# A feed-forward stage with W1 as a seven-product block algorithm and W2 summed in PSUM

## The reference

```python
h = jax.nn.gelu(flat_x @ W1 + b1)          # flat_x 1024 x 512, W1 512 x 2048
y = h @ W2                                 # W2 2048 x 512
y = jnp.nan_to_num(y, nan=0.0, posinf=0.0, neginf=0.0)
return y.reshape(orig_shape) + b2
x = x + _L0_ffn_ref(_layernorm(x, axis=-1), ...)
```

## Time and profile before

| what | value |
|---|---|
| time, median of 3 runs | 2129.53 us (2128.24 to 2131.55) |
| the profiled execution, its own time | 2129.44 us |
| its span, first to last instruction | 2127.5 us |
| mean granted TensorE clock | 0.994 |
| TensorE busy | 2072.3 us, 97% of the span |
| VectorE / ScalarE / GpSimd busy | 1500.6 / 1016.8 / 548.4 us |
| feed-forward products | 1926.20 to 2112.06 us |

### The profile page before, as it was taken

The page is one execution under the profiler, slowest core; times in us unless marked ns, Lnnn a source line. Parts: engine busy times, 40 slices in busy tenths (PEclk is TensorE's granted clock), DMA queues, the critical chain, the costliest instruction groups (busy, mean ns, idle before and its releaser), DMA issues.

```text
span 2127.5 us, 33928 instructions
## 1 busy us (share of the span) xinstructions
PE 2072.3 (97%) x11620; PEld 1785.9 (84%) x11620; DVE 1500.6 (71%) x2365; ACT 1016.8 (48%) x2232; POOL 548.4 (26%) x428
## 2 busy tenths in 40 slices
PE   8999999999999999999899999999999999989996
PEld 6888888888888888888788888888888888877885
DVE  6777777777777777777766666666666666677776
ACT  3555555555555555555544444444444444443331
POOL 2222122212221222221222222222222222213223
PEclk9999999999999999999999999999999999999998
DMA  7000000000000000011011111111111111010111
GB/s 234 16 21 16 15 21 20 15 15 20 20 15 15 20 20 20 10 50 40 31 59 43 42 39 36 40 38 41 42 42 42 42 42 42 23 35 25 49 44 50
DMA packets 44162, 76.90 MB, mean 36 GB/s; under 512 B 7378, under 2 KB 13650, under 8 KB 43602
## 3 DMA queue, kind: packets, MB, share of 16 engines
q1 hardware_dynamic: 44114, 76.25, 11.9%
HBM read 74.13 MB, written 2.10 MB: 36 GB/s over the span
## 4 chain that ended last, share of the span: by engine, by line
PE 87%; DVE 6%; issue 3%; ACT 2%; SPq 1%; DMA 0%; DVEq 0%; ACTq 0%
PE bank L1085 22%; PE bank L1087 21%; PE bank L1086 21%; PE bank L1154 9%; PE bank L1200 6%; PE bank L1268 1%; PE bank L1353 1%; PE bank L1352 1%; PE bank L1269 1%; PE bank L1327 1%; DVE negmax L870 1%; DVE V_lo L864 1%; DVE pT_lo L908 1%; DVE q_lo L902 1%; DVE K_lo L860 0%
## 5 line engine op out<-in xcount | busy, mean ns | idle before, releaser
L880 DVE SCALAR_TENSOR_TENSOR xacc<-bank,rinv,xacc 128x512 f32<-128x512 f32 x512 | 376.1, 746 | 71.1 <-PE bank L1087 71.1
L486 ACT ACTIVATE pT_hi<-bank 128x512 fp32r<-128x512 f32 x320 | 190.7, 597 | 202.5 <-PE bank L1200 202.3
L870 DVE TENSOR_REDUCE negmax<-bank 128x1 f32<-128x640 f32 x256 | 210.2, 822 | 36.7 <-PE bank L1154 29.6
L540 ACT ACTIVATE prob<-bank,negmax 128x640 f32<-128x640 f32 x256 | 202.5, 791 | 66.8 <-DVE negmax L870 66.8
L908 DVE TENSOR_TENSOR pT_lo<-bank,pT_hi 128x512 fp32r<-128x512 f32 x320 | 217.9, 681 | 2.4 <-ACT pT_hi L486 2.4
L1200 PE MATMUL bank<-ident,prob 128*128 128x128 f32 x1280 | 191.3, 272 | 0.0
L1200 PEld LDWEIGHTS bank<-ident,prob 128*128 128x128 f32 x1280 | 159.4, 140 | 19.0
L383 POOL TENSOR_TENSOR wo_lo<-wo_raw,wo_hi 128x512 fp32r<-128x512 f32 x32 | 41.4, 1295 | 430.6 <-ACT wo_hi L486 430.6
L626 ACT ACTIVATE xprob<-xscore,negmax 128x128 f32<-128x128 f32 x256 | 99.5, 391 | 95.2 <-DVE negmax L961 95.2
L1085 PE MATMUL bank<-xwv_hi,cT_hi 128*128 128x256 f32 x512 | 143.4, 280 | 1.4 <-DVE xV_lo L928 1.4
L1086 PE MATMUL bank<-xwv_lo,cT_hi 128*128 128x256 f32 x512 | 143.1, 280 | 0.0
(11 more groups left out here) (171 smaller groups left out, 5909.0 us busy)
## 6 DMA issues: line engine op xcount, KB each, us to landing
wq_raw<-in_wq SPq DMA_DIRECT2D x32, 256.0 KB, 2.6
wo_raw<-in_wo SPq DMA_DIRECT2D x32, 256.0 KB, 2.6
xwv_raw<-in_xwv SPq DMA_DIRECT2D x16, 512.0 KB, 3.5
xwk_raw<-in_xwk SPq DMA_DIRECT2D x32, 256.0 KB, 3.7
xwq_raw<-in_xwq SPq DMA_DIRECT2D x32, 256.0 KB, 3.5
xwo_raw<-in_xwo SPq DMA_DIRECT2D x32, 256.0 KB, 2.7
w_raw<-in_w SPq DMA_DIRECT2D x32, 256.0 KB, 2.6
xacc<-in_x SPq DMA_DIRECT2D x8, 256.0 KB, 5.2
```

The costliest lines, as they stand in the source:

```text
L486: return s.activation(dst, src, ACT.Copy)
L540: s.activation(prob[:, slot, i, :].rearrange("p (a t) -> p a t", a=2), S_bank[i % 2], ACT.Exp, bias=negmax[:, slot, i:i + 1], scale=1.0, a ...
L870: v.tensor_reduce(negmax[:, slot, i:i + 1], S_bank[i % 2], mybir.AxisListType.XY, ALU.max, negate=True).then_inc(a["max"], 1)
L880: v.scalar_tensor_tensor(xacc[:, 4 * half + i, :], M, rinv[:, k, i:i + 1], xacc[:, 4 * half + i, :], ALU.mult, ALU.add).then_inc(sems["y"], 1)
```

## The change

The 1024 tokens are two halves X1, X2 and the 2048 hidden units eight groups (g) of two blocks; the 512 features are two halves of two blocks. The 2x2 block product of a group is made from seven half-size products P1 to P7 (`product`, six matmuls each) in place of eight: 42 matmuls in place of 48. For this the kernel makes sums and differences of the weights on GpSimd (`late_sums`, four operations of 128x256 for a group) and of the transposed x on VectorE (four of 128x1024), and their halves: for each group ScalarE copies a high half of 128x1280 (`late_hi`) and GpSimd makes a low half of 128x1280 (`late_lo`), in two slots. VectorE adds the products: `u2`, `u3`, `u4` and then the four results `c11`, `c21` (first half of the tokens), `c12`, `c22` (second half).

P1 and P2 of four groups are made ahead, while the second half of the layer norm runs. The main part has four groups with P1, P2 of a later group and two blocks of W2 (66 matmuls each), then three of 42 matmuls, then the last.

W2: in the first half of the tokens each block of hidden units is added to four PSUM banks that stay open over all 16 blocks (`y0`); there is no `yacc`. The hidden units of the second half are kept in SBUF (`hid1`), W2 is loaded and split a second time (`again`, `again_hi`, `again_lo`), and the last 192 matmuls go token tile by token tile. W2 has four slots for its halves and two for its raw blocks, and its low halves are made by VectorE (`second_lo`; the first two by GpSimd). The result of a tile is finished by VectorE alone, tile by tile (`finish`). A gelu on one column right after the layer norm's last square root loads the gelu table there. The 16 pieces of b1 are loaded at once; the second `spin` of the stage has 6 calls in place of 18.

```diff
-FUNITS = 2 * NF
+NG = NF // 2
+HALF_S = [0, 1, 2, 3, 4, 6, 8, 10]
+LATE_S = [5, 7, 9, 11, 12, 13, 14, 15]
+Y_ORDER = [0, 2, 4, 6, 8, 1, 10, 3, 12, 5, 14, 7, 9, 11, 13, 15]
...
+            def second(s_):
+                if s_ >= 2:
+                    sp.wait_ge(f["w2hi"], f0["w2hi"] + s_ - 1)
+                    sp.wait_ge(f["w2lo"], f0["w2lo"] + s_ - 1)
+                sp.dma_start(w2_raw[:, s_ % 2], w2[Y_ORDER[s_]]).then_inc(s_w2raw[s_ % 2], 16)
...
+            for g in range(NG):
+                for s_ in (7 + 2 * g, 8 + 2 * g):
+                    if s_ < NF:
+                        second(s_)
+                if g + 5 < NG:
+                    early(g + 5)
+                if g + 2 < NG:
+                    late_weights(g + 2)
+                if g == 4:
+                    sp.wait_ge(f["P2"], f0["P2"] + NG)
+                    for n in range(4):
+                        again(n)
...
+            def late_sums(n):
+
+                w = wl_f[n % 2]
+                pool.wait_ge(s_wlraw[n % 2], 16 * (n // 2 + 1))
+                if n >= 2:
+                    pool.wait_ge(f["wlhi"], f0["wlhi"] + n - 1)
+                    pool.wait_ge(f["wllo"], f0["wllo"] + n - 1)
+                g.tensor_tensor(w[:, 4], w[:, 2], w[:, 3], ALU.add).then_inc(f["S0"], 1)
+                g.tensor_tensor(w[:, 6], w[:, 0], w[:, 2], ALU.subtract)
+                pool.wait_ge(f["S0"], f0["S0"] + 2 * n + 1)
+                g.tensor_tensor(w[:, 5], w[:, 4], w[:, 0], ALU.subtract).then_inc(f["S0"], 1)
+                pool.wait_ge(f["S0"], f0["S0"] + 2 * n + 2)
+                g.tensor_tensor(w[:, 7], w[:, 1], w[:, 5], ALU.subtract).then_inc(f["S"], 1)
+
+            def late_lo(n):
+                pool.wait_ge(f["wlhi"], f0["wlhi"] + n + 1)
+                g.tensor_tensor(wl_lo[:, n % 2], wl_f[n % 2][:, 3:8], wl_hi[:, n % 2], ALU.subtract).then_inc(f["wllo"], 1)
+
...
+            for n in range(NG):
+                if n + 1 < NG:
+                    late_lo(n + 1)
+                if n + 5 < NG:
+                    early_lo(n + 5)
+                if n + 2 < NG:
+                    late_sums(n + 2)
+                if n < 4:
+                    bias(2 * n)
+                    bias(2 * n + 1)
...
+            def second_hi(s_):
+                if s_ >= 4:
+                    act.wait_ge(f["y0"], f0["y0"] + s_ - 3)
+                raw_split(w2_hi[:, s_ % 4], w2_raw[:, s_ % 2], s_w2raw[s_ % 2], 16 * (s_ // 2 + 1), f["w2hi"])
...
+            def late_hi(g):
+                act.wait_ge(f["S"], f0["S"] + g + 1)
+                if g >= 2:
+                    act.wait_ge(f["P4"], f0["P4"] + g - 1)
+                copy(wl_hi[:, g % 2], wl_f[g % 2][:, 3:8]).then_inc(f["wlhi"], 1)
...
+            def p1_copy(g):
+                act.wait_ge(f["P1"], f0["P1"] + g + 1)
+                if g >= 5:
+                    act.wait_ge(f["u4"], f0["u4"] + g - 4)
+                    act.wait_ge(f["u3"], f0["u3"] + g - 4)
+                copy(part[:, g % 5], E_bank[0]).then_inc(f["p1"], 1)
...
+            act.wait_ge(s_b1, 16 * NF)
+            s.activation(nrm[:, 4, 0:1], nrm[:, 1, 0:1], ACT.Gelu_apprx_tanh, bias=b1_sb[:, 0:1], scale=1.0)
...
+            for g in range(NG):
+                if g + 1 < NG:
+                    late_hi(g + 1)
+                for s_ in (5 + 2 * g, 6 + 2 * g):
+                    if s_ < NF:
+                        second_hi(s_)
+                if g + 4 < NG:
+                    p1_copy(g + 4)
+                if g + 1 == NG:
+                    hidden_late(g)
+                hidden_second(g, "c22", "g22", 2 * g + 1, late[:, 2])
+                if g + 4 < NG:
+                    hidden_early(g + 4)
+                if g + 5 < NG:
+                    early_hi(g + 5)
+                hidden_second(g, "c12", "g12", 2 * g, late[:, 1])
+                if g + 1 < NG:
+                    hidden_late(g)
+
...
+            def second_lo(s_):
+                dve.wait_ge(f["w2hi"], f0["w2hi"] + s_ + 1)
+                if s_ == 2:
+                    dve.wait_ge(f["w2lo"], f0["w2lo"] + 2)
+                v.tensor_tensor(w2_lo[:, s_ % 4], w2_raw[:, s_ % 2], w2_hi[:, s_ % 4], ALU.subtract)                 .then_inc(f["w2lo"], 1)
...
+            for g in range(NG - 1):
+                for s_ in (5 + 2 * g, 6 + 2 * g):
+                    if s_ < NF:
+                        second_lo(s_)
+                u2(g)
+                u4(g)
+                u3(g)
+                c22(g)
+                if g + 4 < NG:
+                    c11(g + 4)
+                    h_lo(HALF_S[g + 4])
+                c12(g)
+                c21(g)
+                h_lo(LATE_S[g])
...
+            def finish(b, y):
+                if b >= 2:
+                    dve.wait_ge(f["fin"], f0["fin"] + b - 1)
+                v.tensor_scalar(finite[:, b % 2], y, 0.0, 0.0, ALU.mult, ALU.is_equal).then_inc(f["finite"], 1)
+                if b == 0:
+                    dve.wait_ge(s_xb, B)
+                v.tensor_tensor(ysum[:, b % 2], y, xacc[:, b, :], ALU.add).then_inc(f["sum"], 1)
+                dve.wait_ge(f["finite"], f0["finite"] + b + 1)
+                dve.wait_ge(f["sum"], f0["sum"] + b + 1)
+                v.copy_predicated(xacc[:, b, :], finite[:, b % 2], ysum[:, b % 2]).then_inc(f["fin"], 1)
...
+            def product(dst, w, m):
+                for ch in range(2):
+                    last = mm3(dst, [z[:, ch, :] for z in w], [z[:, ch, :] for z in m], ch == 0, ch == 1)
+                return last
...
+            def p7(g):
+                if g == 0:
+                    pe.wait_ge(f["Tlo"], f0["Tlo"] + 3)
+                if g < 4:
+                    pe.wait_ge(f["u2"], f0["u2"] + g + 1)
+                else:
+                    pe.wait_ge(f["c21"], f0["c21"] + g)
+                product(L_bank, late_w(g, 3), xs(1)).then_inc(f["P7"], 1)
...
+            for g in range(4):
+                fill = 3 if g == 0 else LATE_S[g - 1]
+                p6(g)
+                y0(fill, FIRST)
+                p5(g)
+                p1(g + 4)
+                p7(g)
+                p2(g + 4)
+                p3(g)
+                y0(fill, LAST)
+                p4(g)
+                y0(HALF_S[g + 4], EVERY)
+            p6(4)
...
+            p6(4)
+            for g in range(4, NG - 1):
+                p5(g)
+                p7(g)
+                p6(g + 1)
+                y0(LATE_S[g - 1], FIRST)
+                p3(g)
+                y0(LATE_S[g - 1], LAST)
+                p4(g)
...
+            for t_ in range(4):
+                for n in range(NF):
+                    if n % 4 == 0:
+                        pe.wait_ge(f["g1lo"], f0["g1lo"] + 4 * t_ + n // 4 + 1)
+                    if t_ == 0:
+                        if n % 3 == 2:
+                            pe.wait_ge(f["alo2"], f0["alo2"] + n // 3 + 1)
+                        else:
+                            pe.wait_ge(f["alo"], f0["alo"] + n - n // 3 + 1)
+                    last = mm3(Y1_bank[t_], [z[:, t_ % 2, n, :] for z in (hid1_hi, hid1_lo)],
+                               [z[:, n, :] for z in (w2all_hi, w2all_lo)], n == 0, n == NF - 1)
+                last.then_inc(f["y1"], 1)
```

609 lines of the change are left out of this document (439 added, 170 removed), and 3 rows, old and new, of the table f_after.

## The result

The changed kernel takes 2139.85 us (median of 4 runs, 2138.28 to 2140.75), the kernel before 2129.80 (4 runs, 2128.24 to 2131.55): a ratio of 1.005, with a 95% interval from 1.0038 to 1.0063. It is slower by about 10 us. Forecast were 2137.5 us, in a range from 2121 to 2146.

A forecast was written before the change was run, and what follows sets the result against it. TensorE's matmuls were taken as the bound. Terms -11.2 + 10.3 + 5.7 + 8.0 + 4.6 + 1.4, then -10.2 at the end, gave +8.6 (+8.1 as laid out): 2137.5 us, ratio 1.004, range 2121 to 2146.

The forecast's parts named there:

- The saving of 11.2 us: TensorE in the feed-forward stage: eight groups save 6 matmuls each, 48 x 0.233 us, -11.2 us.
- The end: Behind the last matmul: only one tile left to finish, about 2.2 us in place of 12.46, -10.2 us.
- The port: VectorE operations on two SBUF tiles wait for the GpSimd operation under way, up to 2.97 us for 128x1280.
- short waits: Rival, chance 0.20: VectorE gets through within the 1.24 us that rows show, 2129.5 us, no change.
- The rival with VectorE first at the port: Ramp and groups 1 to 3: VectorE isn't held behind GpSimd, up to 15.7 us less, 2121.8 us, faster; chance 0.25.
- The ramp: Stage start to end of group 0: chained copies, low halves and port waits, P7(0) idle 5.0 us; +10.3 us.
- The early load's price: In the ramp: the early gelu table load on ScalarE makes TensorE wait ahead of P1(1), 1.5 us.
- Groups 1 to 3: P7 waits 1.9 us for u2, behind second_lo and late_lo, in each of three groups; +5.7 us.
- Groups 4 to 6: P6 of the next group waits 3.65 us for late_lo, in groups 5 and 6; with c22's delays +8.0 us.
- The clock: TensorE's clock after the two idle times of 3.65 us: between nothing and 1.4 us each, half taken, +1.4 us.
- a colder clock: Rival, chance 0.10: every wait over 1.8 us costs 1.4 us at half clock; +7.0 us, 2144.5 us.
- The second half: Second half of the tokens: P7(7) waits 0.8 us, W2's reload through four slots adds 3.8 us; +4.6 us.

The follow-up runs named there:

- e11: Changed kernel with GpSimd's late_lo cut into three instructions, P6 waiting for all three; 2132.70 us against 2139.85.
- e6: Changed kernel with GpSimd's late_lo as three instructions, each with its own signal, P6 waiting only for the first; 2121.54 us against 2139.85.
- e4: Changed kernel without the early one-column gelu; 216.95 us from cross-attention's last matmul to the kernel's last, against 218.41.
- e10: e9 without the early one-column gelu that loads the gelu table; median 2110.24 us, against 2111.25.
- e1: Changed kernel with VectorE running u2, u4, u3 and c22 ahead of W2's low halves (second_lo); median 3.1 us shorter, not distinguishable from none.
- e2: Changed kernel with ScalarE's late_hi for groups 6 and 7 ahead of hidden_late; cross-attention's last matmul to the last one 5.2 us shorter.
- e3: Changed kernel with each W2 block (0 to 11) of the second pass used for two row blocks; last cross-attention matmul to last matmul 219.16 us, against 218.41.
- e12: The kernel before, profiled again with no edit; cross-attention's last matmul to the last one 197.36 us, against 198.95 in its first profile.
- e9: e8 with late_lo in three pieces, late block 7 loaded ahead of W2's second pass, and bias additions moved; 2111.25 us, 0.85% less than the kernel before.
- e8: Changed kernel with all reorderings together: VectorE, ScalarE, GpSimd, TensorE and load orders, W2's second pass by two row blocks; 2119.53 us.
- e5: Changed kernel with VectorE's c11(1) ahead of h_lo(0) in the ramp; last cross-attention matmul to last matmul 215.94 us, against 218.41.
- e7: e1 with late W1 blocks loaded before the W2 loads of the same turn; last cross-attention matmul to last matmul 214.04 us.

## Why the prediction was right, point by point

I count the loss as for e11. Before it is 19.2 us from the 36th matmul on and 19.8 at the end (768 matmuls). In the changed kernel:

```
up to matmul             loss, us   more than before   forecast
150 (end of group 0)     25.3        6.0               10.3
348 (groups 1 to 3)      31.6        6.4                5.7
480 (groups 4 to 6)      43.9       12.3                8.0 + 1.4 (clock)
720 (second half)        50.4        6.5                4.6
```

Together 31.2, less 0.6 at the end of before and less 11.2 for the matmuls that are gone: 19.4, the 19.46 of the stretch. Forecast for the last matmul were 18.3.

- **The saving of 11.2 us** is there: 720 matmuls in place of 768.
- **The end**, forecast -10.2, is -10.8.
- **The port.** I took the whole 2.97 us for a wait behind a GpSimd operation of 128x1280, which no row of before showed. It is 2.9, and e6 and e11 show that it ends with the instruction. The rival "short waits" is out by that. The rival with VectorE first at the port is out too: in the ramp h_lo(0) was held to 2.25 us, and in groups 1 to 3 the waits stood; only at 1959 did VectorE go first.
- **The ramp** was forecast 4.3 us too long, and one step in it was wrong: "At 1958.8 `late_lo`(1) has waited longer and runs to 1961.8". VectorE had one operation after another there (1959.06, 1960.19), and `late_lo`(1) took 4.34 us from 1959.36. So W2's low half number 4 ended at 1960.87 and not at 1962.4, and counted from the mark 4.1 us earlier than forecast. The load of block 6 went out at 1960.94, and its high half was ready at 1964.18, just when `late_lo`(1) had let the low half ahead of it go. P7(0) waited 0.94 us, not 5.0. Against this stood the 2.05 us ahead of y0(2) and more half clock (some 4.5 us, 3.0 more than before, where I had 1.2): without the clock the ramp cost 3.0 us, not 9.1. The early load's price, 1.5 us, is not confirmed (e4, e10).
- **Groups 1 to 3**: 1.69, 1.71, 1.70 us idle, which put P7 off by 1.85 each, against 1.9; 0.8 us more is in small gaps. e6 and e11 confirm the cause; e1 shows that the place in VectorE's order alone doesn't give it back, as two other chains (h_lo, the load of block 5) were within 2 us.
- **Groups 4 to 6**: two waits of 3.52 and 3.53 us against 3.65, and e2 confirms the chain. With c22's 0.65 and the starts anew that is the forecast's 8.0; the rest of the 12.3 us is the clock below.
- **The clock** was mis-sized: I took +1.4 us for both waits, from rows after shorter idle times. It was 3.53 us for 8 matmuls (2046.78 to 2050.31, 1.7 lost) and 5.29 us for 12 (2061.90 to 2067.19, 2.5 lost): 4.2. With the ramp the clock took 7.2 us more than before, where I had 2.6. So the mechanism of the rival "a colder clock" was there, though not in its places: in groups 1 to 3 the clock stayed whole (1.00 from 1965 to 2036 us), and it fell behind the 3.5 us and in the ramp.
- **The second half**: P7(7) was put off by 0.9 us against 0.8. For the slots of W2 3.98 us idle look like the forecast's 3.8, but with the six starts anew TensorE was put off by 5.6: this term was 1.8 us too small. e3 shows that the pace of the reload made them.
- **Outside the stage** 2.6 us came on top, which no step of mine had; e12 shows that chance is wide enough for it; whether the new stage has a part in it stays open.
- **Two readings of before** were off without harm: between 1937 and 2112 us TensorE does wait once, 0.62 us ahead of 2108.99 for hid_lo, and at 1978.1 it had done 197 matmuls, not 194. That puts the ramp's term at 11.0; the total was laid out from 1978.1 and doesn't contain it.

The span was forecast at 2135.6 us and is 2138.7: 2.6 outside the stage, 1.2 in the stretch and -0.6 at the end. That it came so near is partly luck. Inside the stretch the waits of the ramp were 6.1 us too dear and the clock 4.6 us too cheap, and these largely cancel; groups 1 to 3 (+0.7) and the second half (+1.9) make most of the rest.

## What to carry to other kernels

A block algorithm that saves matmuls pays with operands that several engines make in series, and its worth is decided by those chains: here 48 matmuls (11.2 us) cost 30.7 us of waits and lost clock in the first order, and 5.5 us (25.3 of loss, less 19.8) in e9's, for the same work. What the seven products are worth by themselves isn't measured: no run has the new W2 and the new end with W1's products as before, and of e9's gain in the span, 15.8 us, 10.8 lie behind the last matmul and 5.7 in the stretch (its mark lies 0.7 later). When a wait is removed and nothing is gained, look at the in-order DMA queue: twice here (e1, e8) the next wait was for a load that was issued late behind loads of other tiles. Cut a long instruction of GpSimd into pieces in the order in which they are used: it signals sooner and lets VectorE at the port.

## What the hardware showed that I had not expected

- Two VectorE operations in a row on SBUF tiles kept GpSimd off the port at 1959 us, though it had waited since the first: 4.34 us for an operation of 2.9. At 53 us of the kernel before the two engines had taken turns. What decides wasn't tried.
- Cutting 128x1280 into three costs little: 3.22 us in all against 2.88 (at 2043.40 in e6), and 4.13 against 3.38 with VectorE's pair beside it, which goes from 4.98 to 2.79 us.
- The same idle time, 1.73 and 1.74 us at the same instruction in two executions of the same kernel, was followed by the full clock (0.39 us a matmul) in one and by half of it (0.63) in the other. After waits of 3.5 us and more it was half in all eight profiles that have such a wait (changed kernel, e1, e3, e4, e5, e7, e8, e11), and after those of 1.62 us in e2 it was whole. In between it goes either way: behind the wait of 1.71 or 1.72 us ahead of P1(1) it was half in seven profiles (changed kernel, e2, e3, e5, e8, e9, e11) and whole in three (e1, e6, e7), and behind 2.69 us it was whole in e9 and fell to half 1 us later in e10.
